# Routed experts: four places for gathered rows, a landing wait among the scatters, and the copy of the next rows ahead of the second half of the gelu

## The chip, the core and the metric

One core of a Trainium2 chip runs the whole program. Its engines work side by side, each through its own list of instructions, and meet only at semaphores: TensorE (PE in the profile) multiplies matrices, VectorE (DVE) and ScalarE (ACT) work elementwise, GpSimd (POOL) issues the indirect DMAs, SyncE (SP) the plain ones. The metric is the device time of one execution in microseconds (us), the median over runs.

## What is computed

The reference is two rounds of a graph network over 6250 nodes of 256 features, each with a layer of experts behind it. All of it is float32:

```python
x = x + _L0_gnn_ref(_layernorm(x), edge_index, ...)      # graph attention
x = x + _L0_ffn_ref(_layernorm(x)[None], ...)[0]         # 8 routed experts, the best 2 for a node
x = x + _L1_gnn_ref(_layernorm(x), src, dst, ...)        # weighted graph sum
x = x + _L1_ffn_ref(_layernorm(x)[None], ...)[0]         # 4 experts, mixed by scores from a second graph
```

The change lies in the second line, whose core is, for each expert `e` with H = 1024:

```python
xe = xn[None] * ln_g[:, None] + ln_b[:, None]
h = gelu(einsum("end,edh->enh", xe, W1) + b1[:, None], approximate=False)
y = einsum("enh,ehd->end", h, W2) + b2[:, None]
out = (weights[:, :, None] * y[its best two experts]).sum(1)
```

The fourth line needs the 131072 edges of a second graph sorted by target. That sorting is a scatter of 1024 columns of 128 pairs of 8 bytes to HBM (`slots`), and it is spread over the earlier stages as work for GpSimd.

## The kernel before

The program is a row of blocks with a barrier behind each. `experts` (L2238) is one of them. The nodes chosen for an expert stand one behind the other in tiles of 128 rows, 105 tiles (NT) in all; `expert_of` tells each tile's expert and `node_of` its rows. The engines run these lists:

- GpSimd (L2304), unrolled over the tiles: for tile t it waits until turn t-2 is done (`tin` at least t-1), gathers the tile's 128 rows of 1 KB into one of two places of XI by an indirect DMA, and then puts five scatters of the sorting (`sort.place`, L612) behind it. `place` goes on counting over the whole program. Before this stage 176 scatters are placed: 16 in the first graph pass, 40 in finish_attention, 15, 55, 20 and 30 in the four stages from the norm to the ordering of the rows. Every eighth scatter waits for those sixteen back. With `pausing` it also waits behind every scatter whose number is 3 modulo 4 until it and all before it on its semaphore have landed; project_nodes (L327) and finish_weighted (L1334) use that, the experts don't.
- SyncE (L2280): loads W1 of each tile (2 x 512 KB) into one of four places, three tiles ahead, behind the store of Y of the tile before; then stores Y.
- TensorE (L2393), for tile t: `by_w1`, the product with W1, 16 products into pH, which signals `h` after each half; `turn_in`, the turning of the rows of tile t+1 (2 transposes into pI), which signals `tin`; `by_w2`, the product of tile t-1 with W2 into pY. The list has the waits for the rows' landing (`s_x`), W1's landing, the turned rows (`xt`), and the gelu.
- ScalarE (L2330), for tile t: the first four gelus (they wait for the first half of `h`), the second four (for the second half), then `copy_in` of tile t+1: two activations that scale the turned rows from pI into XT (they wait for `tin`).
- VectorE (L2353): adds b2 to pY, which makes Y.

Of the kernel before, what the change touches and what calls it, by code (L numbers as in the profile page):

```python
# [28 lines left out]
U32 = mybir.dt.uint32  # L29
# [260 lines left out]
def project_nodes(sh, tag, stats, weight, ncols, att=None, table=None, table_cols=0, keep=None, keep_from=0,  # L290
# [11 lines left out]
    with Scope(nc) as sc:  # L302
# [16 lines left out]
        @block.gpsimd  # L319
        def _(pool):  # L320
            if clear is not None:
                pool.memset(EMPTY[:, :, 0].bitcast(F32), 0.0).then_inc(s_e[0], 1)
                pool.memset(EMPTY[:, :, 1].bitcast(F32), -1.0).then_inc(s_e[0], 1)
            if zero is not None:
                zero_blocks(pool, zero)
            if sort is not None:
                sort.place(pool, count, pausing=True)  # L327
# [263 lines left out]
class EdgeSort:  # L591
# [20 lines left out]
    def place(self, pool, count=NTF, pausing=False):  # L612

        for t in range(self.next, min(NTF, self.next + count)):
            j = t // GRP % 2
            if t >= 2 * GRP and t % GRP == 0:
                pool.wait_ge(self.s_placed[j], t // GRP // 2 * GRP * 16)
            pool.indirect_dma_start(self.slots, bass.IndirectOffsetOnAxis(  # L618
                ap=self.ADDR[:, t:t + 1].bitcast(U32), axis=0), self.PAIR[:, t, :], None).then_inc(self.s_placed[j], 16)
            if pausing and t % 4 == 3:  # L620
                pool.wait_ge(self.s_placed[j], (t // (2 * GRP) * GRP + t % GRP + 1) * 16)
        self.next = min(NTF, self.next + count)
# [681 lines left out]
def finish_weighted(sh, tag, acc, stats, w1t, w2t, b1, b2, sort, count):  # L1304
# [4 lines left out]
    with Scope(nc) as sc:  # L1309
# [22 lines left out]
        @block.gpsimd  # L1332
        def _(pool):
            sort.place(pool, count, pausing=True)  # L1334
# [903 lines left out]
def experts(sh, tag, E, H, ew, expert_of, node_of, rows, ys, y_stored, sort=None, count=0):  # L2238
# [13 lines left out]
    s_x = [sh.lasting_sem(f"{tag}_x{j}") for j in range(2)]  # L2252
    s_w1 = [sh.lasting_sem(f"{tag}_w1_{j}") for j in range(SLOTS)]
    with Scope(nc) as sc:
        W1 = sc.sb(f"{tag}_W1", [P, SLOTS, KC, H])
        XI = sc.sb(f"{tag}_XI", [P, 2, D])
# [48 lines left out]
        def _(pool):  # L2305
            for t in range(NT):
                at_least(pool, s["tin"], t - 1)
                pool.indirect_dma_start(XI[:, t % 2, :], None, rows, bass.IndirectOffsetOnAxis(
                    ap=node_of[:, t:t + 1].bitcast(U32), axis=0)).then_inc(s_x[t % 2], 16)
                sort.place(pool, count)  # L2310

        @block.scalar
        def _(a):
# [16 lines left out]
            def step(rnd, j):  # L2330
# [7 lines left out]
                for c in range(HC):  # L2338
                    if c % BC == 0:
# [3 lines left out]
                if more:  # L2343
                    copy_in(t + 1, 1 - b, e_next)
# [19 lines left out]
        def _(pe):  # L2364
# [28 lines left out]
            def step(rnd, j):  # L2393
                t = rnd * SLOTS + j
                by_w1(t, rnd, j)
                if not isinstance(t, int) or t + 1 < NT:
                    turn_in(t + 1, (j + 1) % 2, rnd * (SLOTS // 2) + (j + 1) // 2 + 1)
# [325 lines left out]
```

## Time and profile before

| | us |
|---|---|
| median of the runs | 8996.98 (8985.14 to 9004.04, 3 runs) |
| the profiled execution | 9013.4 |
| its span, first to last instruction | 9011.7 |
| TensorE busy in the span | 5737.0 (64%) |
| GpSimd busy in the span | 5432.2 (60%) |
| VectorE busy in the span | 3945.5 (44%) |
| ScalarE busy in the span | 1582.5 (18%) |

In the timeline a row is a start, a busy time, an engine, a line of the kernel, an operation with the tile it writes and the tiles it reads, a count, and in brackets the engine's idle time ahead of it with what ended it: an engine and line, a DMA, "issue" (nothing that the profile shows) or "remote" (a signal whose sender the profile can't name). Several instructions of a line are merged into one row. The ends of matmuls are modelled. Of a DMA that GpSimd issues, the row is the issuing alone, not the moving of the data.

### The profile page before, as it was taken

What the parts mean: (1) busy time and instruction counts of PE and PEld (TensorE: products, weight loads), DVE (VectorE), ACT (ScalarE), POOL (GpSimd) and SP (SyncE); (2) the same over time, 40 slices, a digit from 0 to 9 for tenths busy, and PEclk for the clock granted to TensorE, in tenths of its full rate; (3) what the DMA queues carried; (4) which work ended last, traced back from release to release, by engine and by line L of the source; (5) the groups of instructions that cost most, each with busy time, mean ns of one, the idle gap of its engine ahead of it and who ended that gap; (6) DMA issues with size and microseconds to landing.
All of it is one profiled execution on the core that took longest, in us unless ns stands there. A gap on an engine that the chain in (4) does not pass through costs nothing. (4 is left out here: it accounts for less than half of the span.)

```text
span 9011.7 us, 116542 instructions
## 1 busy us (share of the span) xinstructions
PE 5737.0 (64%) x27644; PEld 4852.9 (54%) x27645; DVE 3945.5 (44%) x10109; ACT 1582.5 (18%) x3574; POOL 5432.2 (60%) x5690
## 2 busy tenths in 40 slices
PE   3677777777773488880555444444446588888894
PEld 2555565555553377770343333333335587878783
DVE  4566666777777300005444433343435322222225
ACT  1122222122120233330000000000001233333331
POOL 3666666666665566656666666666666555555562
PEclk7787777787875699995777777676768578788886
DMA  3333333333333244443333222222220222222235
GB/s 111 90 89 88 88 90 87 88 89 88 89 86 101 74 146 143 144 136 112 89 89 89 86 80 79 80 80 80 79 80 21 57 59 63 59 62 61 60 64 164
DMA packets 426058, 793.32 MB, mean 88 GB/s; under 512 B 129162, under 2 KB 267134, under 8 KB 425684
## 3 DMA queue, kind: packets, MB, share of 16 engines
q0 software_dynamic: 235504, 474.87, 20.5%
q1 hardware_dynamic: 190436, 317.20, 10.4%
q8 instruction: 34, 0.56, 0.0%
q14 instruction: 84, 0.69, 0.0%
HBM read 720.67 MB, written 70.98 MB: 88 GB/s over the span
## 5 line engine op out<-in xcount | busy, mean ns | idle before, releaser
L1153 PE MATMUL g_pM<-g_G,g_S 128*128 x3328 | 1215.7, 544 | 1533.6 <-ACTq L1047 999.0
L833 POOL DMA_INDIRECT g_G<-table,X x1664 | 1578.0, 948 | 931.3 <-issue 458.4
L843 POOL DMA_INDIRECT g_G<-table,g_IDX x1616 | 1534.7, 950 | 879.9 <-issue 525.1
L1153 PEld LDWEIGHTS g_pM<-g_G,g_S 128*128 128x128 f32 x3328 | 931.0, 287 | 1818.3 <-issue 1616.1
L1121 PE MATMUL g_pM<-g_G,g_S 128*128 128x260 f32 x3328 | 1261.7, 539 | 697.2 <-DVE acc L950 679.7
L1697 POOL DMA_INDIRECT q_G<-table,slot x1072 | 1035.1, 966 | 724.6 <-issue 272.2
L1121 PEld LDWEIGHTS g_pM<-g_G,g_S 128*128 128x128 f32 x3328 | 826.1, 266 | 989.2 <-DVE acc L950 765.9
L958 DVE TENSOR_TENSOR acc<-g_pM,acc 128x256 f32 x1664 | 695.6, 418 | 1357.7 <-PE g_pM L1153 587.6
L618 POOL DMA_INDIRECT slots<-sort_PAIR,sort_ADDR x1024 | 1014.4, 991 | 455.1 <-issue 294.5
L950 DVE TENSOR_TENSOR acc<-g_pM,acc 128x260 f32 x1664 | 711.7, 428 | 275.3 <-PE g_pM L1121 89.3
L938 DVE TENSOR_SCALAR g_S<-iota,g_REL,g_WT 128x128 f32<-128x128 f32 x1664 | 587.8, 354 | 187.3 <-issue 172.5
L1483 PE MATMUL q_pH<-ew_XT,ew_W 128*128 (+1 forms) x3136 | 564.1, 353 | 136.8 <-ACT ew_GT L1502 121.7
L1483 PEld LDWEIGHTS q_pH<-ew_XT,ew_W 128*128 128x128 f32 x3136 | 525.6, 260 | 158.2 <-ACT ew_GT L1502 120.7
L987 DVE TENSOR_TENSOR g_G<-g_G,g_pF 128x512 f32<-128x512 f32 x832 | 546.0, 677 | 0.3 <-ACT g_pF L1070 0.3
L2380 PE MATMUL e_pH<-e_XT,e_W 128*128 128x128 f32 x3360 | 411.4, 282 | 174.1 <-ACT e_XT L2324 163.4
L2380 PEld LDWEIGHTS e_pH<-e_XT,e_W 128*128 128x128 f32 x3360 | 392.3, 195 | 215.0 <-ACT e_GT L2341 188.7
L1357 ACT ACTIVATE f_XT<-f_pT 128x512 f32<-128x512 f32 x49 | 28.8, 596 | 2676.5 <-PE f_pT L1370 2672.7
L1111 PEld LDWEIGHTS g_pA<-keep,g_ST 128*128 128x128 f32 x3328 | 424.3, 202 | 57.5 <-issue 41.2
L2358 DVE TENSOR_TENSOR e_Y<-e_pY,ew_B 128x256 f32<-128x256 f32 x105 | 44.6, 424 | 937.5 <-PE e_pY L2389 908.8
L1493 PE MATMUL q_pY<-ew_W,ew_GT 128*128 128x256 f32 x1568 | 441.5, 431 | 2.4 <-issue 2.3
L1111 PE MATMUL g_pA<-keep,g_ST 128*128 x3328 | 410.1, 255 | 7.1 <-ACT g_ST L1054 1.2
L2389 PE MATMUL e_pY<-ew_W,e_GT 128*128 x1680 | 381.8, 379 | 0.7 <-DVE e_Y L2358 0.7
(335 smaller groups left out, 6877.4 us busy)
## 6 DMA issues: line engine op xcount, KB each, us to landing
e_W<-in_L_ffn_W SPq DMA_DIRECT2D x210, 512.0 KB
sort_PAIR<-slot_rows SPq DMA_DIRECT2D x66, 512.0 KB
g_G<-table,X POOLq DMA_INDIRECT x1664
g_G<-table,g_IDX POOLq DMA_INDIRECT x1616
ys_all<-ew_Y SPq DMA_DIRECT2D x196, 128.0 KB
sm_Y<-ys_all SPq DMA_DIRECT2D x28, 896.0 KB, 10.7
q_ST<-slot_rows SPq DMA_DIRECT2D x34, 512.0 KB
sort_ADDR<-slot_rows SPq DMA_DIRECT2D x34, 512.0 KB
```

The costliest lines, as they stand in the source:

```text
L618: pool.indirect_dma_start(self.slots, bass.IndirectOffsetOnAxis(ap=self.ADDR[:, t:t + 1].bitcast(U32), axis=0), self.PAIR[:, t, :], None). ...
L833: pool.indirect_dma_start(G[:, r, u, :], None, table, bass.IndirectOffsetOnAxis(ap=IDX[:, k * GRP + u:k * GRP + u + 1].bitcast(U32), axis= ...
L843: pool.indirect_dma_start(G[:, r, u, :], None, table, bass.IndirectOffsetOnAxis(ap=IDX[:, g * GRP + u:g * GRP + u + 1].bitcast(U32), axis= ...
L938: v.tensor_scalar(S[:, r, u, :], sh.iota[:, :], rel, WT[:, bass.ds(k * GRP + u, 1)], ALU.is_equal, ALU.mult).then_inc(s["onehot"], 1)
L950: v.tensor_tensor(node_sums(blk), pM[u % BANKS][:, 0:width], node_sums(blk), ALU.add).then_inc(s["added"], 1)
L958: v.tensor_tensor(node_sums(blk), pM[r % 2 * 2 + u // HG][:, u % HG, :], node_sums(blk), ALU.add).then_inc(s["added"], 1)
L1111: m = pe.matmul(pA[:, r % 2, u, :], ST[:, u, :], nodes, start=True, stop=True)
L1121: m = pe.matmul(pM[u % BANKS][:, 0:width], S[:, r, u, :], G[:, r, u, :], start=True, stop=True)
L1153: m = pe.matmul(pM[r % 2 * 2 + half][:, u % HG, :], S[:, r, u, :], rows.rearrange("p a d -> p (a d)"), start=True, stop=True)
L1483: m = pe.matmul(self.pH[e % n][:, c, :], self.W1[:, e, k, c * P:(c + 1) * P], self.XT[:, bass.ds(i, 1), k, :].rearrange("p a m -> p (a m)" ...
L1697: pool.indirect_dma_start(G[:, r, u, :], None, table, bass.IndirectOffsetOnAxis(ap=node_of_slot[:, 2 * (k * GRP + u):2 * (k * GRP + u) + 1 ...
L2380: m = pe.matmul(pH[j % 2][:, c, :], W1[:, j, k, c * P:(c + 1) * P], XT[:, j % 2, k, :], start=(k == 0), stop=(k == KC - 1))
```

## The change

XI gets four places instead of two, with four semaphores, and the gather of tile t waits for turn t-4. `place` takes a number instead of a flag, and the experts pass their 5: a wait for landing behind each scatter whose number is 4 modulo 5. ScalarE copies the next tile's turned rows ahead of the second four gelus. TensorE takes the rows from the four places.

```diff
--- before.py
+++ after.py
@@ -324,7 +324,7 @@
             if zero is not None:
                 zero_blocks(pool, zero)
             if sort is not None:
-                sort.place(pool, count, pausing=True)
+                sort.place(pool, count, pause_every=4)
 
         @block.sync
         def _(sp):
@@ -609,7 +609,7 @@
         ap = self.sh.X[:, block:block - (-n // D), :].rearrange("p i d -> p (i d)")[:, 0:n]
         return ap if dt == F32 else ap.bitcast(dt)
 
-    def place(self, pool, count=NTF, pausing=False):
+    def place(self, pool, count=NTF, pause_every=0):
 
         for t in range(self.next, min(NTF, self.next + count)):
             j = t // GRP % 2
@@ -617,7 +617,7 @@
                 pool.wait_ge(self.s_placed[j], t // GRP // 2 * GRP * 16)
             pool.indirect_dma_start(self.slots, bass.IndirectOffsetOnAxis(
                 ap=self.ADDR[:, t:t + 1].bitcast(U32), axis=0), self.PAIR[:, t, :], None).then_inc(self.s_placed[j], 16)
-            if pausing and t % 4 == 3:
+            if pause_every and t % pause_every == pause_every - 1:
                 pool.wait_ge(self.s_placed[j], (t // (2 * GRP) * GRP + t % GRP + 1) * 16)
         self.next = min(NTF, self.next + count)
 
@@ -1331,7 +1331,7 @@
 
         @block.gpsimd
         def _(pool):
-            sort.place(pool, count, pausing=True)
+            sort.place(pool, count, pause_every=4)
 
         @block.scalar
         def _(a):
@@ -2249,11 +2249,11 @@
     W2, B2, VT = ew.W2, ew.B2, ew.VT
     w1_rows = ew.src[0].rearrange("e (c p) n -> (e c) p n", p=P)
     s = {n: sh.sem(f"{tag}_{n}") for n in ("tin", "xt", "h", "gelu", "y", "yc")}
-    s_x = [sh.lasting_sem(f"{tag}_x{j}") for j in range(2)]
+    s_x = [sh.lasting_sem(f"{tag}_x{j}") for j in range(SLOTS)]
     s_w1 = [sh.lasting_sem(f"{tag}_w1_{j}") for j in range(SLOTS)]
     with Scope(nc) as sc:
         W1 = sc.sb(f"{tag}_W1", [P, SLOTS, KC, H])
-        XI = sc.sb(f"{tag}_XI", [P, 2, D])
+        XI = sc.sb(f"{tag}_XI", [P, SLOTS, D])
         XT = sc.sb(f"{tag}_XT", [P, 2, KC, P])
         GT = sc.sb(f"{tag}_GT", [P, 2, HC, P])
         Y = sc.sb(f"{tag}_Y", [P, 2, D])
@@ -2304,10 +2304,10 @@
         @block.gpsimd
         def _(pool):
             for t in range(NT):
-                at_least(pool, s["tin"], t - 1)
-                pool.indirect_dma_start(XI[:, t % 2, :], None, rows, bass.IndirectOffsetOnAxis(
-                    ap=node_of[:, t:t + 1].bitcast(U32), axis=0)).then_inc(s_x[t % 2], 16)
-                sort.place(pool, count)
+                at_least(pool, s["tin"], t - SLOTS + 1)
+                pool.indirect_dma_start(XI[:, t % SLOTS, :], None, rows, bass.IndirectOffsetOnAxis(
+                    ap=node_of[:, t:t + 1].bitcast(U32), axis=0)).then_inc(s_x[t % SLOTS], 16)
+                sort.place(pool, count, pause_every=count)
 
         @block.scalar
         def _(a):
@@ -2336,12 +2336,12 @@
                     e, = expert(a, regs[0:1], t)
                 at_least(a, s["y"], t - 1)
                 for c in range(HC):
+                    if c == HC - BC and more:
+                        copy_in(t + 1, 1 - b, e_next)
                     if c % BC == 0:
                         a.wait_ge(s["h"], t * (HC // BC) + c // BC + 1)
                     a.activation(GT[:, b, c, :], pH[b][:, c, :], ACT.Gelu,
                                  bias=VT[:, 0, bass.ds(e * HC + c, 1)]).then_inc(s["gelu"], 1)
-                if more:
-                    copy_in(t + 1, 1 - b, e_next)
 
             over_tiles(a, step)
 
@@ -2394,7 +2394,7 @@
                 t = rnd * SLOTS + j
                 by_w1(t, rnd, j)
                 if not isinstance(t, int) or t + 1 < NT:
-                    turn_in(t + 1, (j + 1) % 2, rnd * (SLOTS // 2) + (j + 1) // 2 + 1)
+                    turn_in(t + 1, (j + 1) % SLOTS, rnd + (j + 1) // SLOTS + 1)
                 if not (isinstance(t, int) and t == 0):
                     e, = expert(pe, regs, t - 1)
                     by_w2(t - 1, (j + 1) % 2, e)
```

## Rows read from the trace of the kernel before

**Rows 1.** Timeline, tiles 1 and 104: start, busy, engine, line, [idle before]
```profile
3107.56 6.03 PE L2380 MATMUL e_pH<-e_XT,e_W 128*128 128x128 f32 x32 [12.44 <-ACT e_XT L2324]
...
4049.54 3.73 PE L2380 MATMUL e_pH<-e_XT,e_W 128*128 128x128 f32 x32
```

**Rows 2.** Groups by line, 3107.5 to 4042: count | busy, mean ns | idle before
```profile
L618 POOL DMA_INDIRECT slots<-sort_PAIR,sort_ADDR x510 | 489.7, 960 | 155.4 <-issue 155.4
...
L2380 PE MATMUL e_pH<-e_XT,e_W 128*128 128x128 f32 x3264 | 397.9, 281 | 170.8 <-ACT e_XT L2324 162.1 <-issue 6.3 <-ACT e_GT L2341 2.2
...
L2341 ACT ACTIVATE e_GT<-e_pH,ew_VT 128x128 f32<-128x128 f32 x816 | 232.2, 368 | 631.0 <-remote 463.2 <-PE e_pH L2380 145.1 <-issue 22.6
...
L2308 POOL DMA_INDIRECT e_XI<-rows,node_of x102 | 100.7, 988 | 190.5 <-remote 167.5 <-issue 16.0 <-PE e_pI L2371 7.0
```

**Rows 3.** Timeline of one steady tile
```profile
3499.07 0.99 POOL L2308 DMA_INDIRECT e_XI<-rows,node_of  x1 [1.77 <-remote]
...
3500.86 3.83 PE L2380 MATMUL e_pH<-e_XT,e_W 128*128 128x128 f32 x32 [1.58 <-ACT e_XT L2324]
...
3504.53 0.38 PE L2371 MATMUL e_pI<-ident,e_XI 128*128 128x128 f32 x2
...
3504.75 3.62 PE L2389 MATMUL e_pY<-ew_W,e_GT 128*128 x16
...
3505.43 0.96 POOL L618 DMA_INDIRECT slots<-sort_PAIR,sort_ADDR  x1 [0.31 <-issue]
...
3507.98 1.14 ACT L2341 ACTIVATE e_GT<-e_pH,ew_VT 128x128 f32<-128x128 f32 x4 [0.47 <-remote]
...
3508.16 1.00 POOL L2308 DMA_INDIRECT e_XI<-rows,node_of  x1 [1.78 <-remote]
...
3508.52 0.42 DVE L2358 TENSOR_TENSOR e_Y<-e_pY,ew_B 128x256 f32<-128x256 f32 x1 [8.57 <-PE e_pY L2389]
...
3508.99 0.82 ACT L2324 ACTIVATE e_XT<-e_pI,ew_VT 128x128 f32<-128x128 f32 x2
...
3509.95 3.83 PE L2380 MATMUL e_pH<-e_XT,e_W 128*128 128x128 f32 x32 [1.58 <-ACT e_XT L2324]
```

**Rows 4.** Timeline at the end of the stage, behind GpSimd's last scatter
```profile
4038.81 0.96 POOL L618 DMA_INDIRECT slots<-sort_PAIR,sort_ADDR  x1 [0.30 <-issue]
...
4042.22 3.81 PE L2380 MATMUL e_pH<-e_XT,e_W 128*128 128x128 f32 x32 [1.96 <-issue]
...
4046.16 1.14 ACT L2341 ACTIVATE e_GT<-e_pH,ew_VT 128x128 f32<-128x128 f32 x4 [0.58 <-PE e_pH L2380]
```

**Rows 5.** Timeline around a gather that came late
```profile
3408.27 0.99 POOL L2308 DMA_INDIRECT e_XI<-rows,node_of  x1 [3.21 <-issue]
...
3417.01 1.14 ACT L2341 ACTIVATE e_GT<-e_pH,ew_VT 128x128 f32<-128x128 f32 x4 [5.05 <-remote]
...
3418.98 1.28 PE L2380 MATMUL e_pH<-e_XT,e_W 128*128 128x128 f32 x6 [2.85 <-ACT e_XT L2324]
```

**Rows 6.** Timeline of an earlier stage whose scatters have the wait
```profile
2880.16 0.95 POOL L618 DMA_INDIRECT slots<-sort_PAIR,sort_ADDR  x1 [5.21 <-DMA slots<-sort_PAIR,sort_ADDR]
...
2909.41 0.96 POOL L618 DMA_INDIRECT slots<-sort_PAIR,sort_ADDR  x1 [0.30 <-issue]
...
2911.39 0.38 ACT L424 ACTIVATE p_XT<-p_pT 128x256 f32<-128x256 f32 x1 [1.01 <-PE p_pT L437]
...
2911.78 0.96 POOL L618 DMA_INDIRECT slots<-sort_PAIR,sort_ADDR  x1 [1.41 <-DMA slots<-sort_PAIR,sort_ADDR]
```

**Rows 7.** Stretches: busy us (count) by engine, granted clock, DMA share, GB/s
```profile
2874.00:2880.00 6.00, 5.95 (x29) 5.24 (x29) 4.42 (x19) 1.92 (x5) 0.95 (x1) 0.50 1.08 354
...
2909.40:2911.80 2.40, 2.40 (x14) 2.40 (x14) 1.92 (x12) 0.77 (x2) 0.98 (x2) 0.50 0.02 1
```

**Rows 8.** The same columns, two stretches of the steady tile
```profile
3502.00:3504.00 2.00, 2.00 (x21) 2.00 (x20) 0.00 (x0) 0.00 (x0) 1.55 (x2) 1.00 0.89 225
...
3506.00:3508.00 2.00, 2.00 (x11) 1.73 (x10) 0.00 (x0) 1.16 (x5) 0.38 (x1) 1.00 0.03 7
```

## The prediction

> **What bounds the kernel now.** The kernel is a row of stages with barriers between them, and the change touches one: the routed experts, L2238, 105 tiles of 128 gathered rows. I read the stage by line, then one tile in the timeline, then the places where the pattern breaks. It runs from about 3080 to 4062 us; from tile 1's first matmul (3107.56) to tile 104's (4049.54) are 103 tiles, 9.146 us each [rows 1].
>
> By line, TensorE's stall is "ACT e_XT", 162.1 us: it waits for the next tile's turned rows. ScalarE waits 463.2 us for "remote", a signal whose sender the profile doesn't name, and GpSimd's gather waits 167.5 us for "remote" too [rows 2]. So everybody seems to wait for somebody. The timeline of one tile resolves it [rows 3]. W1's product takes 3.83 us, the turn of the next rows 0.38, W2's product of the tile before 3.62, one behind the other: 7.65 us less overlaps, from 3500.86 to 3508.37. Then TensorE stands for 1.58 us. The turn ended at 3504.91 and W1's product at 3504.69, yet the second half of the gelu starts only at 3507.98 and the gather that waits for the turn at 3508.16, both over 3 us late. The bias add of Y starts at 3508.52, 0.15 us behind its matmul. TensorE's results are there, but some of its signals are late.
>
> What holds them is seen where GpSimd is quiet. Its last scatter starts at 4038.81. The tile at 4042.22 then has its second gelu half at 4046.16, 0.1 us behind the product, and the next tile begins after 7.32 us [rows 1, 4]. In the steady tile it comes 2.55 us after the start of the last scatter of the run (3505.43 to 3507.98). And where one gather was 1.44 us late for a reason of its own (idle 3.21 instead of 1.77 or 1.78), the second gelu half came at 3417.01, 8.74 us after that gather, against 8.91 us in the steady tile (3499.07 to 3507.98), and TensorE stood 2.85 instead of 1.58 us [rows 3, 5]. So I read the stage as a ring that runs through GpSimd: gather, five scatters, signals released, which let the next gather go. Worked out: gather to scatter 0.99 + 0.30 = 1.29; four steps between scatters of 0.96 + 0.30 = 1.26 each [rows 2, 3], 5.05; last scatter to the next gather 2.73 (3505.43 to 3508.16). Sum 9.07, against 9.09 from gather to gather. GpSimd's 1.6 to 1.8 us of idle time are a link of this ring, not slack, and ScalarE's order of work hardly matters to it.
>
> **The change part by part.** (1) *Four places for XI.* The gather of tile t waits for turn t-4 and no longer t-2, two tiles further back, so GpSimd never stands for it as long as it is the slowest; the last link, 2.73 us, falls out of the ring and an ordinary step of 1.26 takes its place. It adds two semaphores and 2 KB a partition, no instruction. Alone it would remove the only gap in GpSimd's run, in which the signals pass; the next part puts one back.
>
> (2) *A wait for landing.* The condition is on the scatter's number, and 176 scatters stand before the stage, so the wait falls behind the fourth of a tile's five (number 179, 184, ...), then one scatter, then the next gather. Queued behind it on GpSimd are that scatter and all later gathers; for those TensorE waits. Its price is in an earlier stage that has this wait: with DMA engines at 0.02 the idle time is 1.41 us, 2.37 us from start to start; at a DMA share of 1.08 it is 5.21, 6.17 from start to start [rows 6, 7]. These are the two ends. In that stage ScalarE, waiting for TensorE, got its signal at 2911.39, within the wait, 1.98 us behind the last scatter's start (2909.41) [rows 6]: the gap does let the signals out. Which end holds here? W1 of a tile (1 MB) fills the queues from about 1 to 5 us behind the W1 product's start (3500.86): DMA share 0.89 in 3502 to 3504, 0.03 in 3506 to 3508 [rows 8]. It is issued behind the store of Y, so behind W2's end. In the new ring call the release R. The last scatter starts 0.4 us after it at the latest, the gather at about R + 1.4 to 1.7, the four scatters up to R + 6.5 to 6.8, and their packets move later still. The product starts at R + 1.1 (below), W2 ends at R + 8.6, at about the next release, and W1 moves from there + 3 to + 7.4. The fourth scatter's data goes then at about + 8: just behind it. So I take the quiet end, 2.37, plus an allowance of 0.08 for the tiles where the load is still there. New ring: 1.29 + 3 x 1.26 + 2.37 + 1.26 = 8.70, say 8.72 with the rounding of the rows; with the allowance and 0.05 for late gathers like the one in [rows 5], less what the last tiles gain, 8.85 a tile.
>
> The Trainium skill's page "DMA: Bandwidth & Descriptors", section "Anatomy of one DMA — SWDGE (gpsimd) path", gives such a DMA a fixed cost of about 2.0 us, most of it the receipt of the last write, and its section "Latency and other measured facts" says that HBM's access takes 0.2 us on average and 2 us at high load. The row at rest (2.37 from the start of the instruction) agrees with the first; by the second the ring could be some 1.8 us longer, an estimate from that page, which is the slow rival below.
>
> (3) *Copy ahead of the second half of the gelu.* No instruction more or less: two copies (3508.99 to 3509.81, 0.82 us) go ahead of four gelus whose starts are 1.01 us apart in all (3507.98 to 3508.99) [rows 3]. Both halves wait for signals released together, so the next product could start 1.0 us sooner after the release: at R + 1.1 instead of R + 2.1. The delayed gelus end at about R + 2.0, and W2 reads them at R + 5: covered. In the ring it gives nothing, since TensorE is not on it. It keeps TensorE's own path, 1.1 + 7.5 = 8.6 us, just inside 8.72; without it that would be 9.6 us, still only one release a tile. I count it at 0.
>
> (4) *Start.* Eight loads of 512 KB open the stage, and the gather of tile 1 lands behind them. Tile 1's product starts only at 3107.56, and TensorE stood 12.44 us for it [rows 1], all but the last microseconds behind unbroken runs of scatters. With the wait the gather of tile 1 goes about 4 us later, its landing hardly (it stands behind W1 either way), and the release comes behind the fourth scatter after it, at about 3100: product at about 3101, 6 us sooner.
>
> Sum: 103 x (9.146 - 8.85) = 31, plus 6, is 37 us. The profiled execution took 9013.4 us (span 9011.7), the median of the runs is 8996.98; the stage is the same in both as far as can be told, so I take 37 from each: 8976 for a profiled one and **8960** for the median, -0.41%. All other edits (the number instead of a flag at two other calls) leave their instructions as they are: 0.
>
> **Rivals.** (a) *The ring goes as worked out*: 8960. With no allowance at all it is 8.72 a tile, 44 + 6 = 50 us: 8947. With 0.3 more it is 8991. Chance 0.68 for this family, of which nearly all is faster by over 0.2%.
> (b) *The wait is paid at the loaded price.* If W1's transfers move into the fourth scatter's time, the wait grows from 1.41 towards 5.21 us. The change breaks even where it is 1.8 us (9.15 - 0.05 - 6.33 - 0.96, the ring without the wait being 6.33). With a quarter of the way to the loaded row (2.4 us), a tile is 9.7 us, the stage 57 us longer less 6: 9048. For it: W1 and scatters share the engines, and the margin above is about half a microsecond. Against: a longer ring puts W1 earlier before the wait, so the two move apart by themselves. Chance 0.14.
> (c) *Nothing is gained.* The release may need more than the gap gives: it came 2.55 us behind the last scatter in this stage [rows 3], 1.98 in the one with waits [rows 6], and the new gap is 2.37. Signals missed in one gap cost part of a ring now and then, and 6 tiles that lose a whole 8.7 us would eat the 37 us: about 8997. Chance 0.12.
> (d) *TensorE's late signals are its own*, not GpSimd's doing. The profile's ends of matmuls are modelled, and the skill's page "Perfetto Trace Analysis", section "Tensor Engine Instruction (MATMUL, LD_WEIGHTS)", says the end is estimated and the signal follows PSUM's acknowledgement. Then part 3 counts, 1.0 us a tile, and the tile would be 8.15 us: 8997 - 103 - 6, 8888. But GpSimd's own 8.72 a tile stands in the way of it in any case, which leaves (a)'s number; only if the wait ended much before 2.37 us could it come out, and [rows 4] speak against the premise. Chance 0.06.
>
> **The numbers.** The time is that of (a). The range takes (a) with its floor and some of (d), and (c) and the lighter part of (b): 8930 to 9010. A difference under 0.2% (18 us) can't be told from none in this kernel: faster 0.70, same 0.15, slower 0.15.
>
> **What the profile after would show.** Tile to tile 8.7 to 8.9 us; GpSimd's wait for "remote" in front of the gather gone and a wait for the landing of slots in front of every fifth scatter, near 1.41 us each, 105 of them; the two copies ahead of the second gelu half; TensorE still waiting for the copy, some 1.2 us a tile; tile 1 starting near 3101. Step 2 is wrong if that landing wait is over 1.8 us in the mean, the ring is wrong if the tile is under 8.6 us or if GpSimd still waits for turns, and step 1's gap is too short if single tiles of 17 us appear.

## The result and the profile after

The changed kernel took 9043.43 us (9036.02 to 9057.09, 4 runs), the kernel before 8991.06 (8984.1 to 9004.04, 4 runs): ratio 1.0061, 95% interval 1.0046 to 1.0076. It is slower by 0.6%, where 0.4% faster was forecast. The profiled execution took 9043.98 us with a span of 9042.2, against 9013.4 and 9011.7 before.

The experts account for it. From TensorE's first instruction in them to the last of all they took 976.5 us before and 1035.1 after, 58.6 more. The combine behind them is 8.1 us shorter, and the pass over the sorted slots near the end (from 7131 us before) 28.7 us; that pass has no edit, and in all the traces below it takes anywhere between 1702 and 1750 us on chips like this one, so it is taken as variation between executions. The stage behind the second graph pass, up to the next norm, is 6.3 us longer, and no other differs by over 3 us. What follows is about the 58.6.

Timeline of the kernel after, first matmul of tile 1 and of tile 104, then GpSimd's last gather and VectorE's last addition:

```profile
3096.76 5.21 PE L2380 MATMUL e_pH<-e_XT,e_W 128*128 128x128 f32 x30 [1.20 <-ACT e_XT L2324]
...
4107.60 3.73 PE L2380 MATMUL e_pH<-e_XT,e_W 128*128 128x128 f32 x32
...
4076.20 1.00 POOL L2308 DMA_INDIRECT e_XI<-rows,node_of  x1 [0.30 <-issue]
...
4119.37 0.42 DVE L2358 TENSOR_TENSOR e_Y<-e_pY,ew_B 128x256 f32<-128x256 f32 x1 [4.00 <-PE e_pY L2389]
```

Against [rows 1], tile 1 starts 10.8 us sooner and tile 104 58.1 us later: (4107.60 - 3096.76) / 103 = 9.81 us a tile instead of 9.15. The first gathers of the two kernels start at 3079.83 after and 3080.85 before; the last ones at 4076.20 and 4032.45. So GpSimd alone brings 44.8 us of the loss (9.58 us from gather to gather). The rest comes behind its last gather: 43.6 us to the end of the stage (4076.20 to 4119.8), 29.2 before. With four places TensorE can be two tiles further behind GpSimd, and at the end it was.

The groups by line, kernel after, 3107.5 to 4042 (count | busy, mean ns of one | idle time ahead, with what ended it):

```profile
L618 POOL DMA_INDIRECT slots<-sort_PAIR,sort_ADDR x489 | 469.4, 960 | 326.9 <-DMA slots<-sort_PAIR,sort_ADDR 190.1 <-issue 136.8
L2380 PE MATMUL e_pH<-e_XT,e_W 128*128 128x128 f32 x3040 | 408.0, 298 | 123.8 <-ACT e_XT L2324 121.3 <-issue 2.2
...
L2343 ACT ACTIVATE e_GT<-e_pH,ew_VT 128x128 f32<-128x128 f32 x756 | 216.4, 379 | 426.7 <-remote 275.3 <-PE e_pH L2380 142.0 <-issue 9.3
L2308 POOL DMA_INDIRECT e_XI<-rows,node_of x98 | 96.9, 988 | 42.6 <-issue 23.1 <-remote 16.9 <-PE e_pI L2371 2.6
...
L2358 DVE TENSOR_TENSOR e_Y<-e_pY,ew_B 128x256 f32<-128x256 f32 x95 | 40.4, 425 | 917.6 <-PE e_pY L2389 456.1 <-remote 396.8 <-issue 64.7
```

Beside [rows 2]: GpSimd's wait for the turn has gone from 167.5 to 16.9 us, nearly as forecast, and a wait for the scatters' landing has come, 190.1 us. Up to the end of the stage it is 202.2 us in 92 waits, 2.2 us each, where the break-even was 1.8. New, and in no step of the forecast, is VectorE's row: it waited 396.8 us for a signal whose sender the profile doesn't name. That is the end of W2's product, whose signal before was at most 1 us late (890.1 us of VectorE's wait are "PE e_pY", none "remote").

One stretch of the timeline shows both (kernel after; columns as in [rows 3]):

```profile
3652.54 3.62 PE L2389 MATMUL e_pY<-ew_W,e_GT 128*128 x16
...
3655.80 0.96 POOL L618 DMA_INDIRECT slots<-sort_PAIR,sort_ADDR  x1 [0.30 <-issue]
3658.16 0.96 POOL L618 DMA_INDIRECT slots<-sort_PAIR,sort_ADDR  x1 [1.40 <-DMA slots<-sort_PAIR,sort_ADDR]
3658.33 0.81 ACT L2324 ACTIVATE e_XT<-e_pI,ew_VT 128x128 f32<-128x128 f32 x2 [6.36 <-remote]
...
3661.27 0.42 DVE L2358 TENSOR_TENSOR e_Y<-e_pY,ew_B 128x256 f32<-128x256 f32 x1 [11.74 <-remote]
...
3665.43 1.43 SPq L2286 DMA_DIRECT2D e_W<-in_L_ffn_W  x2
...
3668.65 0.96 POOL L618 DMA_INDIRECT slots<-sort_PAIR,sort_ADDR  x1 [3.18 <-DMA slots<-sort_PAIR,sort_ADDR]
```

W2's product ends at 3656.16, inside the gap in GpSimd's transfers (3655.80 to 3658.16, 2.36 us). The trace also keeps the time at which each semaphore changed: that of the second half of W1's product, ended at 3652.49, at 3657.38, that of the turn, ended at 3652.71, at 3658.10, both within the gap. W2's, the last of the three, came only at 3661.14, 5 us behind the product's end, and VectorE adds Y at 3661.27. The store of Y and the next load of W1 hang on it, and the load's packets then lie over the next fourth scatter: its wait is 3.18 instead of 1.40 us. The DMA share over the two waits:

```profile
3655.80:3658.10 2.30, 0.36 (x2) 0.00 (x0) 0.00 (x0) 0.00 (x0) 0.96 (x1) 1.00 0.02 1
3664.50:3668.60 4.10, 2.57 (x9) 1.79 (x9) 0.00 (x0) 1.50 (x6) 0.96 (x1) 0.91 0.63 189
```

Tiles of 17 us, which the forecast named as the sign of a gap too short, are there: three of them from 3129 to 3182. Their TensorE also runs at the lower granted clock behind its stalls: the W1 product of 3164.75, behind a stall of 4.43 us, takes 6.10 us, against 3.83 us in [rows 3], and the granted clock over it is 0.61, mostly the lower of the two levels (1.2 GHz), against 1.00 in [rows 8]:

```profile
3164.75:3170.85 6.10, 6.10 (x33) 5.97 (x33) 0.42 (x1) 0.89 (x4) 3.77 (x5) 0.61 0.11 25
```

From 3100 to 4000 the granted clock is 0.93 after, 0.98 to 0.99 before.

### The profile page after: what moved, and what is told of

It is laid out like the page before. It is cut to its first block and busy times, and to the rows that moved or that the text cites. A ratio compares the mean times of both kernels' runs of the same rounds, so it can differ in the third digit from the quotient of the medians.

```text
span 9042.2 us, 116531 instructions
## 1 busy us (share of the span) xinstructions
PE 5817.6 (64%) x27644; PEld 4920.2 (54%) x27645; DVE 3947.5 (44%) x10109; ACT 1578.2 (17%) x3574; POOL 5440.0 (60%) x5690
## 5 line engine op out<-in xcount | busy, mean ns | idle before, releaser
L2380 PE MATMUL e_pH<-e_XT,e_W 128*128 128x128 f32 x3360 | 452.1, 299 | 131.6 <-ACT e_XT L2324 126.0
L2380 PEld LDWEIGHTS e_pH<-e_XT,e_W 128*128 128x128 f32 x3360 | 438.6, 213 | 161.9 <-issue 152.1
L1111 PEld LDWEIGHTS g_pA<-keep,g_ST 128*128 128x128 f32 x3328 | 425.3, 202 | 62.0 <-issue 46.7
L2389 PE MATMUL e_pY<-ew_W,e_GT 128*128 x1680 | 402.8, 389 | 28.1 <-issue 26.2
```

The lines of the kernel that those rows point to most:

```text
L1111: m = pe.matmul(pA[:, r % 2, u, :], ST[:, u, :], nodes, start=True, stop=True)
L2380: m = pe.matmul(pH[j % 2][:, c, :], W1[:, j, k, c * P:(c + 1) * P], XT[:, j % 2, k, :], start=(k == 0), stop=(k == KC - 1))
```

## Experiments

All ratios are to the kernel before, run beside it on the same chip. "A tile" is the mean over the 103 tiles from tile 1's first matmul to tile 104's; "spread" is the standard deviation of their lengths. The runs are in five groups on five chips, numbered 2 to 6 here (whether one of them is the chip of the first comparison isn't known), and the chips differ, which the second group brought to light.

### The parts alone (chip 2; the kernel before took 9018.48 us)

The parts are those of the diff: four places; the landing wait (the number 5 to `place`); the copy ahead of the second half of the gelu.

**places_only**

> Only the four places for XI; no landing wait in the experts, no copy ahead of the gelu. Theory A (the places set GpSimd free of TensorE's turns, and a release of signals that falls beside GpSimd's gap is held until the next one): GpSimd's train of six instructions runs at its own rate of 1.29 + 5 x 1.26 = 7.59 us a tile until it is two tiles further ahead, then stands for a turn again, and the ring goes on as before at about 9.1 us a tile: within 20 us of the kernel before, with the stage's first tiles irregular. Theory B (the loss in the changed kernel is only that the fourth scatter lands behind W1's transfers, 2.2 us a wait): the places are harmless, so no change here either, or a gain, but no tiles of 13 us and more in this run. A tile over 13 us here speaks for A, none for B.

Measured: 9038.87 us, ratio 1.0014 (0.9992 to 1.0036). 9.21 a tile, one of 20.1 us, spread 1.17. Gather to gather 9.15 us, as before. The wait for the turn is back: "remote 162.9" us against 167.5 in [rows 2].

**pause_only**

> Only the landing wait behind the fourth scatter of a tile's five; two places for XI, the order of ScalarE as before. Theory A: with two places the gather still waits for the turn two tiles back, which keeps GpSimd's train in step with TensorE, so each release falls in a gap; the landing wait is then a second gap in the ring, and no tile takes over 13 us. The ring is between 8.7 us a tile (the gather finds its turn there: 45 us faster than before) and 1.1 us above before (9.15 + 1.11, both gaps paid: 110 us slower). Theory B: what the wait costs is set by W1's transfers and not by the places: a mean of 2.2 us a wait, tile 9.6 to 9.9 us, 45 to 75 us slower than before, as in the changed kernel.

Measured: 9072.5 us, 1.0058 (1.0041 to 1.0075). 9.74 a tile, spread 1.43, up to 16.0 us. The landing wait, from its groups by line, 3130 to 4040:

```profile
L618 POOL DMA_INDIRECT slots<-sort_PAIR,sort_ADDR x472 | 453.2, 960 | 318.4 <-DMA slots<-sort_PAIR,sort_ADDR 188.4 <-issue 130.0
```

**order_only**

> Only the copy of the next tile's rows ahead of the second half of the gelu. Theory A and B alike: TensorE is not on the ring through GpSimd, so nothing is gained or lost, within 15 us of before; TensorE's next product starts 1.0 us sooner behind the released signal, and its W2 product then waits longer for it. If TensorE were on the ring (the forecast's rival d) it would be 1.0 us a tile, 103 us faster.

Measured: 9021.46 us, 0.9991 (0.997 to 1.0011); 9.16 a tile.

**pause_order**

> The whole change but for the four places: two places for XI, landing wait, copy ahead of the gelu. Theory A: the four places are what costs the changed kernel its time, so without them the stage has no tile over 13 us, and this kernel is at least 30 us faster than the changed one (9043). Theory B: it takes the same time as the changed kernel within 20 us, and the wait for landing stays at 2.2 us in the mean.

Measured: 9064.04 us, 1.0052 (1.0032 to 1.0071); 9.66 a tile, spread 1.56, up to 17.0 us; mean landing wait 2.09 us. From its last gather (4079.09) to the end of the stage (4105.5) it has 26.4 us, the changed kernel 43.6.

What follows: the tile of 20.1 us in places_only spoke for theory A, but the theory falls with the two others. Without the four places the long tiles stay and the loss stays (1.0052 and 1.0058 against 1.0061). The landing wait by itself brings the loss. The four places cost some 17 us at the end of the stage, and by themselves one long tile near its start (the stage is 14 us longer in places_only than in order_only, 991.8 against 977.7); neither is clear of noise in the time of the whole. The copy's place is worth nothing that can be told, so rival (d) is out.

### Whether W1's packets make the wait long (chip 3; before took 8638.23 us)

The edit of both W1 kernels:

```diff
+                n = H if isinstance(t, int) and t < SLOTS else H // 8
                 for c in range(KC):
-                    sp.dma_start(W1[:, j, c, :], w1_rows[...]...).then_inc(s_w1[j], 16)
+                    sp.dma_start(W1[:, j, c, 0:n], w1_rows[...]...[:, 0:n]).then_inc(s_w1[j], 16)
```

**after_w1_small**

> The changed kernel with the transfers of W1 cut to an eighth from the fifth tile on: 128 of 1024 columns of each row, so 2 KB instead of 16 KB a partition and tile in the same eight DMAs; the products use stale weights for the rest. Theory B (the landing wait is long because W1's packets are in the queues when the fourth scatter lands): the wait falls to 1.41 to 1.45 us in the mean (2.1 in the changed kernel), GpSimd goes from gather to gather in 8.72 us, the stage is 85 us shorter than in the changed kernel (1035 to about 950) and 25 to 30 us shorter than in the kernel before. Theory C (the wait is short of the time in which the third signal of TensorE, the end of W2, gets out, and that alone makes the tiles irregular): the wait falls as well, but tiles of over 13 us stay and the stage is still longer than before's 976 us.

(The load is in fact two DMAs and 8 KB a partition and tile, cut to 1 KB.) Measured: 8761.59 us, 1.0144 (1.0127 to 1.0161). 8.82 a tile, spread 0.63; landing wait 1.47 us.

**before_w1_small**

> The kernel before with the transfers of W1 cut to an eighth from the fifth tile on in the same way. It has no landing wait in the stage. Theories B and C: the ring of 9.07 us (gather, five scatters, 2.73 us until the turn's signal lets the next gather go) has no transfer of W1 in it, so the stage stays at 9.0 to 9.1 us a tile and loses only the late gathers and the start: 960 to 977 us. If it falls below 8.9 us a tile, W1's transfers are in the ring of the kernel before too.

Measured: 8638.08 us, 0.9999 (0.999 to 1.0009). 7.62 a tile, spread 0.18, where 9.0 to 9.1 was expected. Its groups by line, 3060 to 3780:

```profile
L618 POOL DMA_INDIRECT slots<-sort_PAIR,sort_ADDR x473 | 454.2, 960 | 144.2 <-issue 144.2
L2342 ACT ACTIVATE e_GT<-e_pH,ew_VT 128x128 f32<-128x128 f32 x756 | 215.5, 368 | 437.7 <-PE e_pH L2381 437.7
L2309 POOL DMA_INDIRECT e_XI<-rows,node_of x94 | 93.0, 989 | 28.7 <-issue 28.7
```

No "remote" on ScalarE, where [rows 2] have 463.2 us, and none on GpSimd. This isn't W1's doing, since before_load_first, with its whole loads, has 7.67 a tile on the same chip, and the unedited kernel takes 8638 us there. On this chip the signals of TensorE aren't held. GpSimd's six instructions run without a gap, 1.29 + 5 x 1.26 = 7.59 us, which is what the forecast's ring comes to without its last link. The stage ahead, which orders the rows, takes 46.7 us here and 78.1 in the first trace, with thirty scatters in both.

**after_load_first**, SyncE's order turned round:

```diff
                     load(t - 1 + SLOTS, (j - 1) % SLOTS, ex)
-                sp.wait_ge(s["yc"], t + 1)
-                sp.dma_start(ys[bass.ds(t * P, P), :], Y[:, j % 2, :]).then_inc(y_stored[j % 2], 16)
+                if not (isinstance(t, int) and t == 0):
+                    store(t - 1, (j - 1) % 2)
```

> The changed kernel with SyncE's order turned round: W1 of a later tile is issued as soon as its slot is free (end of the product that read it), and the store of Y of the tile before behind it, where in the changed kernel the load waits behind the store of Y and so for the signal of W2's end. Theory B with C (that signal is often held until the next gap, and the load that hangs on it then moves during the landing wait): the load now moves right behind the release, from 1.3 to 6 us behind it, and is through when the fourth scatter lands. Landing wait 1.4 to 1.7 us in the mean, 8.75 to 9.0 us a tile, 60 to 85 us faster than the changed kernel, 10 to 30 us faster than before. If the load's place doesn't matter (only its amount does), it stays at 2.1 us a wait and within 15 us of the changed kernel.

Measured: 8835.96 us, 1.0233 (1.0216 to 1.025). 9.56 a tile, spread 2.55, landing wait 2.20 us.

**before_load_first**

> The kernel before with SyncE's order turned round in the same way: W1's load ahead of the store of Y. Nothing in its ring through GpSimd waits for either, so within 0.2% of before. It could lose if the load now moves while the scatters' descriptors wait, with no wait for landing here to show it: not expected.

Measured: 8635.25 us, 0.9995 (0.9985 to 1.0004); 7.67 a tile.

What follows: on such a chip a landing wait has no held signals to let out and is pure loss. Even the quiet one costs 1.2 us a tile (8.82 - 7.62, where 1.41 - 0.30 = 1.11 is the wait above an ordinary step). Whether W1's packets and not the signals are the loss on the first kind of chip was open still.

### The same on chips that hold the signals (chip 4; before took 8888.57 us)

**after_again**, the changed kernel

> The changed kernel itself, once more, beside the kernel before on whatever chip this is. The runs so far show two kinds of chip: one on which the kernel before takes about 9000 us and TensorE's signals are held while GpSimd issues its indirect transfers (9.1 us a tile), and one on which it takes 8638 us, no signal of TensorE is late and a tile takes 7.6 us, the pace of GpSimd's six instructions. Theory H (what the change costs depends on that): on a chip of the first kind the ratio to before is 1.005 to 1.007 as at first; on one of the second kind there is no gap to be put in place of, the whole landing wait of 1.1 to 1.8 us above an ordinary step is added to each of 105 tiles, 115 to 190 us, ratio 1.013 to 1.022. If the change cost the same on both kinds, it would be 50 us and 1.006 on the second kind too.

Measured: 8935.15 us, 1.0049 (1.0033 to 1.0064). 9.67 a tile, spread 1.49; ScalarE's gelu waited 263.3 us for "remote". A chip of the first kind; the changed kernel itself was never run on one of the other kind.

**after_w1_small_2**

> The changed kernel with the transfers of W1 cut to an eighth from the fifth tile on (128 of 1024 columns; the products use stale weights for the rest), once more beside the changed kernel. On a chip that holds the signals: if the load behind which the fourth scatter lands is the whole loss (theory B), the wait is 1.41 to 1.5 us and the tile 8.7 to 8.9 us, 25 to 45 us faster than the kernel before; if signals that miss the short gap cost by themselves (theory C), the wait is short and the kernel is no faster than before. On a chip that does not hold them: 1.0144 to before again, and the changed kernel above it by 0.6 to 0.7 us a tile, 60 to 75 us.

Measured: 8902.99 us, 1.0018 (1.0003 to 1.0033). First and last product, and groups by line from 3060 to 3780:

```profile
3027.97 5.25 PE L2381 MATMUL e_pH<-e_XT,e_W 128*128 128x128 f32 x23 [1.20 <-ACT e_XT L2325]
...
3984.66 3.73 PE L2381 MATMUL e_pH<-e_XT,e_W 128*128 128x128 f32 x32
...
L618 POOL DMA_INDIRECT slots<-sort_PAIR,sort_ADDR x400 | 384.0, 960 | 217.0 <-issue 110.3 <-DMA slots<-sort_PAIR,sort_ADDR 106.8
...
L2359 DVE TENSOR_TENSOR e_Y<-e_pY,ew_B 128x256 f32<-128x256 f32 x77 | 32.7, 425 | 691.6 <-PE e_pY L2390 340.8 <-remote 279.4 <-issue 71.5
```

The landing wait is down from 2.09 to 1.49 us, the stage from 1021.2 to 981.5, 39.7 us. But it is 9.29 a tile with spread 1.84 and tiles up to 15.9 us, and still no faster than the kernel before: both theories have a share. VectorE's "remote" is there with the load gone.

### A longer gap (chip 5; before took 8903.5 us)

**after_third**, the changed kernel

> The changed kernel itself, as the one that the other runs of this call are compared with. On a chip that holds TensorE's signals: 1.004 to 1.008 to before. On one that does not (before near 8640 us): 1.013 to 1.022, since each landing wait is then added in full.

Measured: 8964.15 us, 1.0094 (1.0051 to 1.0137); 9.69 a tile, spread 1.44. One of its five executions, 9046.56 us at a granted clock of 0.687 where the others had 0.764 to 0.767, pulls the ratio up: by the medians it is 1.0068.

**after_w1_small_longer**

```diff
                 pool.wait_ge(self.s_placed[j], (t // (2 * GRP) * GRP + t % GRP + 1) * 16)
+                if idle is not None:
+                    pool.memset(idle[0], 0.0).then_inc(idle[1], 1)
+                    pool.wait_ge(idle[1], (t - 179) // 5 + 1)
```

> The same longer gap in the kernel whose transfers of W1 are cut to an eighth from the fifth tile on (the products use stale weights for the rest), so that the landing wait is 1.41 us and nothing but the gap's length is changed. Beside the 9.29 us a tile, with spread 1.8 us and tiles of 12 to 16 us, that this kernel had with the short gap: theory C expects 9.3 to 9.4 us a tile with a spread under 0.7 us; theory D 9.9.

Measured: 8927.65 us, 1.0031 (1.0017 to 1.0046). 9.39 a tile, spread 0.44. The gap is 0.54 us longer (2.03 us between two transfers instead of 1.49), yet only 0.10 us a tile more than with the short one, and the tiles are regular. Its groups by line, 3060 to 3780:

```profile
L2348 ACT ACTIVATE e_GT<-e_pH,ew_VT 128x128 f32<-128x128 f32 x612 | 174.3, 372 | 135.6 <-PE e_pH L2385 110.1 <-issue 25.5
...
L623 POOL MEMSET e_IDLE<- 128x512 f32 x78 | 40.9, 524 | 94.4 <-DMA slots<-sort_PAIR,sort_ADDR 94.4
...
L2363 DVE TENSOR_TENSOR e_Y<-e_pY,ew_B 128x256 f32<-128x256 f32 x77 | 32.7, 424 | 687.7 <-PE e_pY L2394 687.7
```

No wait for "remote" on VectorE, and none ahead of the gelu (ScalarE's copy still has 338.3 us of it: the turn's signal comes out in the gap, once a tile). W2's semaphore is never over 0.30 us behind the product's end here; with the short gap 43 of the 105 additions started over 1 us behind it. Theory C holds: 2.37 us from start to start is too short a gap, 2.96 is enough. In its steady tile the turn's copy starts at 3407.18 and VectorE at 3407.25, 2.5 us behind the fourth scatter's start (3404.69), in the part by which the gap was lengthened.

**after_longer**, the same with the whole W1

> The changed kernel with a memset of 128x512 on GpSimd behind each landing wait (0.55 to 0.65 us by the profile's row of 342 ns for 128x260), so that the gap in its indirect transfers is 0.6 us longer. Theory C (the gap of 2.37 us is too short: W2 ends or its signal gets out just behind it, is then held until the next gap, and TensorE loses more than the gap): on a chip that holds the signals the tiles become regular, none over 13 us, and although GpSimd's own work is 0.6 us a tile more, the stage is no longer than the changed kernel's, or shorter by up to 30 us. Theory D (GpSimd's pace alone sets the stage and TensorE's late signals cost nothing beyond it): 0.6 us x 105 = 63 us slower than the changed kernel. On a chip that does not hold them: 60 us slower in any case.

Measured: 9017.44 us, 1.0131 (1.0101 to 1.0161). 10.29 a tile, spread 2.82, up to 15.0 us. The hope that the tiles become regular falls, and 53 us above after_third (the stage 62 us longer, 1084.7 against 1022.5) is what theory D expected. But the signals are better here too: 14.1 us of "remote" ahead of the gelu against 202.4 in after_third in the same window, and none on VectorE against 305.1. What lengthens the tile is GpSimd's own round: 10.26 us from gather to gather against 9.46 in after_third, and TensorE is hardly behind it any more (10.29 a tile against 10.26, where after_third has 9.69 against 9.46). The memset comes on top of a landing that is as long as before, 2.09 us in the mean against 2.11. In the 51 tiles where the load's queue is idle behind the scatter it is 1.2 us, in the 49 where it is busy most of the time about 3, and the two alternate. So the longer gap cures the signals and leaves the other half as it was: with the whole load the pace of GpSimd sets the tile, as theory D has it.

**after_load_first_2**

> The changed kernel with W1's load issued ahead of the store of Y of the tile before, on SyncE, so no longer behind the signal of W2's end. On a chip that holds the signals, theory B (place of the load): landing wait 1.5 to 1.8 us instead of 2.1, 30 to 60 us faster than the changed kernel. If it stays within 15 us, the place of the load in SyncE's queue is not what makes it meet the landing. On a chip that does not hold them it was 1.0233 to before.

Measured: 8955.74 us, 1.0055 (1.0032 to 1.0079); landing wait 2.05 us. Within 15 us of after_third. The load's place in SyncE's queue is not what brings it into the wait: whether behind Y or behind W1's product, it hangs on a signal of TensorE. That both come out with the release, so that the load moves at much the same time, is the likely reason; it wasn't tested.

### Whether the ring is what sets the tile (chip 6; before took 8997.26 us)

**no_scatters**: the experts get 0 instead of 5.

> The kernel before with no scatters in the experts; the 525 of them are issued in one run behind the second graph pass instead, where nothing hides them. If TensorE's signals are held only while GpSimd issues indirect transfers back to back, one gather every 7 us holds nothing: no signal is over 1.5 us late, every tile takes 7.2 to 7.4 us on any chip, and the stage is 760 to 785 us. The rest costs 525 x 1.26 = 660 us, so the whole is 450 to 480 us slower on a chip that holds signals, near 600 on one that does not. If a chip of the first kind holds signals for another reason, the tile stays above 8 us.

Measured: 9450.12 us, 1.0508 (1.0473 to 1.0544). 7.25 a tile, spread 0.01; the whole 453 us slower, where 450 to 480 was expected. Windows, 3150 to 3800, TensorE busy without a pause at full clock:

```profile
3150.00:3800.00 650.00, 650.00 (x4491) 613.04 (x4490) 37.94 (x90) 267.97 (x900) 85.03 (x90) 1.00 0.50 181
```

Chip 6 is of the first kind (before near 9000 us, the ordering of the rows 78.6 us), and in this stage no signal is late.

**four_scatters**

```diff
-            experts(sh, "e0", 8, 1024, ew, expert_of, node_of, rows[0], ys, y_stored, sort, 5)
+            experts(sh, "e0", 8, 1024, ew, expert_of, node_of, rows[0], ys, y_stored, sort, 4)
...
-                       sort=sort, place=130, tail=8, src_tiles=a["src_t"], tables=tables)
+                       sort=sort, place=200, tail=43, src_tiles=a["src_t"], tables=tables)
```

> The kernel before with four scatters a tile instead of five; of the 105 left over 70 go one each into groups of the second graph pass and 35 behind it. The ring (gather 1.29, three steps of 1.26, 2.73 until the turn's signal) would be 7.81 us. TensorE's path from one release to the next is 2.1 + 7.5 = 9.6 us there, so the ring cannot close that fast if both matter: 7.8 to 8.6 us a tile on a chip that holds signals, 55 to 135 us less in the stage, against 132 us more in the graph pass, where GpSimd has no time left: between 25 us faster and 80 us slower in all. If the ring is not what sets the tile there, it stays above 9 us. On a chip that does not hold signals: 7.3 us a tile (TensorE), 33 us less, 132 more.

Measured: 8988.8 us, 0.9996 (0.998 to 1.0011). 7.76 a tile, spread 0.22:

```profile
3097.05 5.25 PE L2380 MATMUL e_pH<-e_XT,e_W 128*128 128x128 f32 x23 [10.36 <-ACT e_XT L2324]
...
3896.42 3.73 PE L2380 MATMUL e_pH<-e_XT,e_W 128*128 128x128 f32 x32
```

The ring's arithmetic gave 7.81. The experts are 146 us shorter than in the first trace (830.5 against 976.5), more than the 55 to 135 expected. From the end of the combine to the start of finish_weighted, which takes in the second graph pass and the scatters behind it, it is 2739.6 us against 2597.4 in no_scatters, 142 more for 105 scatters, and so the whole is the same.

**four_order**, with the copy ahead of the second half of the gelu

> The same four scatters, with the copy of the next tile's rows ahead of the second half of the gelu. TensorE's path from release to release is 1.0 us shorter (8.6 us). If that path is what holds four scatters above 7.81 us a tile, this is 0.3 to 1.0 us a tile faster than four_scatters, 30 to 100 us; if the ring alone sets the tile, no difference. On a chip that does not hold signals: no difference.

Measured: 8982.25 us, 0.9981 (0.9963 to 0.9999); 7.74 a tile. TensorE's path behind a release doesn't matter there. It is the only version whose interval lies below the kernel before, by 0.2%, at the edge of what can be told; on a chip that holds no signals the 105 moved scatters should cost more than the 0.3 us a tile down to TensorE's own 7.25 give back, which wasn't run.

## Why the prediction was wrong

**The ring: right.** The profile was read rightly where it mattered most. One scatter less took 1.39 us off the tile (9.15 to 7.76; 1.26 by the sum, on another chip), none at all left TensorE at 7.25 with no late signal, and on the chip without held signals the tile is the 7.6 us of GpSimd's instructions. The floor of 8.72 us for the new ring was seen as well: the shortest gather to gather after is 8.71.

**Four places: right that the turn falls out, wrong that it is harmless.** The wait for the turn went. What wasn't counted is that two more tiles of lead can be lost at the end: 43.6 us from last gather to end instead of 29.2.

**The landing wait: the step that failed.** It was sized at 1.41 + 0.08 us of idle time; it is 2.1 to 2.2. The step put the fourth scatter's data just behind the load of W1, with a margin of about half a microsecond, and took the quiet price for it. The trace of the changed kernel shows that this is not quiet. Over 103 waits (all but those of the first two tiles), by the share of the 2 us up to the fourth scatter's start in which packets of the plain DMAs' queue, the load's and the store's, were moving: under 5%, 29 waits, 1.43 us in the mean; 5 to 30%, 18 waits, 1.51; over 30%, 56 waits, 2.70. So a load that runs until shortly before the scatter already goes with a long landing, and by the forecast's own placing (load from R + 3 to R + 7.4, scatter at R + 6.5 to 6.8) it lies in those 2 us. The argument that "a longer ring puts W1 earlier before the wait, so the two move apart by themselves" was the wrong one: load and scatter move apart for a tile, the wait is short again, and GpSimd's train comes back onto the load a tile or two later. Short and long waits take turns; they don't settle on the quiet end. With the load cut, the wait is 1.49 us, within 0.01 of the forecast's allowance, and 40 us of the stage go. GpSimd's own round shows how much of the loss goes through this wait: without it the ring is 6.33 + 0.96, with the mean wait of 2.13 us that is 9.42 of the 9.58 us from gather to gather, where the forecast's wait of 1.49 would make 8.78. That is 0.64 x 104 = 67 us.

The Trainium skill's page "DMA: Bandwidth & Descriptors", section "Anatomy of one DMA — SWDGE (gpsimd) path", gives a fixed cost of about 2.0 us. The quiet landing agrees with it (2.37 us from start to start); the loaded one, 2.70 + 0.96 = 3.66 us from start to start in the mean, decided here.

**The gap's length: rival (c), at the same time.** Forecast as an alternative with 6 tiles lost, it is a steady loss. The release was known to need 2.55 us in this stage [rows 3] and 1.98 in the earlier one [rows 6]; the gap gave 2.37, and the forecast built on the shorter. With the load cut but the gap short, a tile is 9.29 us, where the forecast, with the same wait of 1.49 us, had 8.85; 0.44 x 103 = 45 us, about as much as the load's 40. The two can't simply be added in the changed kernel, since a late signal of W2 moves the load as well. The price of (c) was also made too small by counting whole rings lost. A third of the tiles lose a piece: in the changed kernel VectorE starts over 1 us behind W2's end in 35 of 105 tiles, by 4.9 us in the mean of those. The next W2 waits for Y, and the turn of the tile after it can miss its gap.

So the forecast's 1.49 us of wait became 2.1 for (b), its 8.85 us a tile became 9.29 for (c) even with the load cut, and the two feed each other. Rival (b)'s 9048 us is near the measured 9043 with a tile of 9.7 against 9.81, but for half of its reason. The two were weighed as exclusive, 0.14 and 0.12, though one margin of some tenths of a microsecond stood behind both. That is where 0.70 for "faster" was too much: two margins, 0.5 us for the load and 0.4 to -0.2 for the release, had to hold in 105 tiles of 105.

**The copy: right, 0** (0.9991, 0.997 to 1.0011). **The start: better than forecast**, tile 1 at 3096.76 instead of 3101, 10.8 us gained, and lost in the tiles of 17 us that follow.

**Rival (d): out**, by order_only and by no_scatters, and by the times of the semaphores. In the tile of [rows 3] W1's product ends at 3504.70 and its signal comes at 3507.86, while in no_scatters none of TensorE's signals in this stage is over 0.02 us behind the modelled end.

What stays open: what makes a chip hold the signals, why a load ahead of the scatter lengthens its landing, and whether the gap must be longer than 2.37 us by 0.1 or by 0.5; only 0.54 to 0.59 was tried.

## What to carry to other kernels

GpSimd's wait for the turn was a gap of the right length by itself: it ended when the held signal came. A wait for something unrelated, here a landing, ends when that is done, and its length has to be right in every round. So when a wait on a signal is exchanged for a wait of fixed length, compare its length with the latest release that the trace shows, not with the earliest, and price it with the busiest row of the queue it waits on unless the two are tied together. And one count of a resource in the loop, one scatter fewer, moved the tile by about its step in the ring, as no rearrangement of waits here did; the scatters then cost as much where they were put.

## What the runs showed of the hardware

**Chips differ in whether TensorE's signals are held while GpSimd issues indirect transfers back to back.** Four of the five chips and that of the first comparison did it, with the kernel before at 8889 to 9018 us; one did not, at 8638, 3 to 4% less, without one late signal in the experts. The times of the semaphores show it directly: in the kernel before 103 of 104 recorded signals of the turn come over 1 us behind the modelled end of the matmul, 3.0 us in the median, while none of ScalarE's and VectorE's in this stage is over 0.02 us late; in before_w1_small on the other kind of chip no signal of TensorE is either. On the holding chips a held signal comes out about 2.5 us behind the start of the last transfer (2.48 in the median for the turn's in the kernel before, nine in ten by 2.52), or several microseconds late within a run of them, as W2's at 3661.14 above.

**A GpSimd instruction that isn't a transfer lets them out:** the memset of 0.52 us behind the wait counts as part of the gap (in after_w1_small_longer the turn ended at 3402.93 and its held signal let ScalarE start at 3407.18, while the memset ran from 3406.85 to 3407.37).

**One scatter's landing** is 2.37 us from start to start in quiet and up to 4.9 us beside a tile's 1 MB of loads in this stage (idle 3.91), 6.17 in the earlier stage of [rows 6].

**A single change had ratios of 1.0049, 1.0061 and 1.0094 in three comparisons** on chips of the same kind (1.0068 by the medians in the third). For an effect of this size the kernel before has to run beside it on the same chip.
